# Message passing with a segment maximum: 32 of 731 row gathers taken over by TensorE's products with one-hots

## The reference

```python
x_src = x[src]; x_dst = x[dst]                       # x 6250x256 f32, 100000 edges, sorted by dst
theta_x = (x_dst - x_src) @ theta_w.T + theta_b
phi_x = x_src @ phi_w.T + phi_b
e = relu(theta_x + phi_x)
out = segment_max(e, dst, num_segments=6250)         # nodes without edges: 0
x = layernorm(x + where(isfinite(out), out, 0.0))
```

## Time and profile before

| | |
|---|---|
| median of 3 runs | 1252.21 us (1241.03 to 1252.56) |
| the profiled execution's own time | 1256.27 us |
| its span, from the first to the last instruction | 1254.5 us |
| mean granted TensorE clock | 0.574 of full speed |
| moved by DMA | 245.77 MB, 196 GB/s |

### The profile page before, as it was taken

One profiled execution on the slowest core, in us unless ns is written; L12 is line 12 of the kernel. 1 busy time (PEld: TensorE's weight loads), 2 busy tenths in 40 slices (PEclk: granted clock), 3 DMA queues, 4 the chain that ended last, 5 costly groups with the idle time before them and its releaser, 6 DMA issues.

```text
span 1254.5 us, 5930 instructions
## 1 busy us (share of the span) xinstructions
PE 302.1 (24%) x942; PEld 190.4 (15%) x953; DVE 507.1 (40%) x1155; ACT 278.6 (22%) x576; POOL 805.5 (64%) x840
## 2 busy tenths in 40 slices
PE   4165222333243323200000000010023442440000
PEld 3154111222132212100000000000011221220000
DVE  4001323455243434633334343354322542544498
ACT  1022222333232323321112121122100110111134
POOL 6713756766666667677656766767765657657574
PEclk9578555666555656555555555555555765655555
DMA  6467545666465656766656565677654756747264
GB/s 205 146 218 232 183 133 181 219 208 214 148 217 183 202 176 218 242 226 201 195 164 205 190 204 189 213 231 243 194 184 157 239 189 202 243 154 244 93 194 157
DMA packets 111585, 245.77 MB, mean 196 GB/s; under 512 B 19141, under 2 KB 51226, under 8 KB 111546
## 3 DMA queue, kind: packets, MB, share of 16 engines
q0 software_dynamic: 39984, 109.21, 30.8%
q1 hardware_dynamic: 71130, 135.51, 29.4%
q10 hardware_dynamic: 432, 0.66, 0.2%
HBM read 129.89 MB, written 115.45 MB: 196 GB/s over the span
## 4 chain that ended last, share of the span: by engine, by line
another core or an unknown queue 29%; DVE 27%; issue 21%; POOL 9%; PE 8%; ACT 4%; DMA 3%; DVEq 1%; SPq 0%; ACTq 0%; POOLq 0%
DVE acc L553 15%; POOL rows L299 9%; DVE hist L553 5%; PE ps_b L407 2%; ACT hist L359 2%; DVE stats L640 1%; DVE a_sb L629 1%; DVE hist L637 1%; PE acc L391 1%; DVE reached L559 1%; DVE a_sb L624 1%; PE ps_a L442 1%; PE ps_a L391 1%; DMA rows<-b_table,idx 1%
## 5 line engine op out<-in xcount | busy, mean ns | idle before, releaser
L299 POOL DMA_INDIRECT rows<-b_table,idx x731 | 700.0, 958 | 390.4 <-issue 216.2
L359 ACT COPY hist<-acc 128x512 f32<-128x512 f32 (+1 forms) x261 | 151.7, 586 | 497.9 <-DVE hist L553 247.1
L553 DVE SCALAR_TENSOR_TENSOR acc<-acc,reset,rows 128x256 f32<-128x256 f32 x260 | 128.2, 493 | 126.9 <-issue 46.6
L553 DVE SCALAR_TENSOR_TENSOR hist<-acc,reset,rows 128x256 f32<-128x256 f32 x261 | 126.3, 484 | 87.9 <-DVE acc L553 40.7
L553 DVE SCALAR_TENSOR_TENSOR acc<-hist,reset,rows 128x256 f32<-128x256 f32 x209 | 102.8, 492 | 136.3 <-issue 36.7
L407 PE MATMUL ps_b<-diff_sb,conv_t 128*128 128x256 f32 x204 | 89.5, 583 | 228.7 <-ACT conv_t L350 132.5
L427 PE MATMUL ps_d<-hi,row_of 128*128 128x270 bf16 (+1 forms) x89 | 43.3, 487 | 365.4 <-remote 195.7
L442 PE MATMUL ps_a<-theta_sb,xt_sb 128*128 128x256 f32 x196 | 78.3, 552 | 141.6 <-issue 89.4
L407 PEld LDWEIGHTS ps_b<-diff_sb,conv_t 128*128 128x128 f32 x204 | 52.5, 285 | 247.3 <-ACT conv_t L350 136.3
L553 DVE SCALAR_TENSOR_TENSOR acc<-hist,reset,early 128x256 f32<-128x256 f32 x51 | 25.2, 495 | 151.9 <-ACT hist L359 123.6
L364 ACT ACTIVATE signs<-ps_d,node_up 128x782 bf16<-128x782 f32 x49 | 44.7, 913 | 143.2 <-issue 72.3
(11 more groups left out here) (104 smaller groups left out, 313.7 us busy)
## 6 DMA issues: line engine op xcount, KB each, us to landing
runmax<-hist SPq DMA_DIRECT2D x260, 384.0 KB
rows<-b_table,idx POOLq DMA_INDIRECT x731
b_table<-rows SPq DMA_DIRECT2D x7, 896.0 KB, 5.5
xt_sb<-in_xt SPq DMA_DIRECT2D x49, 128.0 KB
early<-in_x SPq DMA_DIRECT2D x12, 512.0 KB
out<-hist SPq DMA_DIRECT2D x11, 512.0 KB, 2.9
xt_sb<-in_xt SPq DMA_DIRECT2D x7, 512.0 KB
xt_sb<-in_xt SPq DMA_DIRECT2D x7, 384.0 KB
```

What stands on the lines that cost most here:

```text
L299: pool.indirect_dma_start(out=rows[:, PLACE[k], :], out_offset=None, in_=b_table, in_offset=bass.IndirectOffsetOnAxis(ap=idx[:, k:k + 1], ...
L359: nc.scalar.copy(hist[:, slot:slot + n - 1, :], acc[:, at:at + n - 1, :]).then_inc(s_copied, 1)
L553: nc.vector.scalar_tensor_tensor(new, former, reset[:, k:k + 1], row_at(k), ALU.min, ALU.max).then_inc(s_fold, 1)
```

## The change

One step in 32 groups (the first step of each) is no longer gathered. It is worked out by TensorE as a product of one-hots with the table. For that the table is read back from HBM into SBUF in 25 loads of two tiles during the groups 0 to 24 and split into three bfloat16 parts whose sum is the float32 value: ScalarE rounds the first part, VectorE subtracts it, ScalarE rounds the second, VectorE subtracts that (two operations of 128x512 on each of the two engines for each load).

There are 8 products of four steps each. For a product, the 512 source numbers of its four steps are loaded to all partitions and made int16 by ScalarE. For each of the 49 tiles VectorE compares them with the tile's node numbers (128x512, int16 in, bfloat16 out), with four buffers for one-hots, and TensorE multiplies: two halves by three parts, 6 matmuls of 512 columns for each one-hot, accumulated in the two `ps_a` banks. The 49 one-hots are spread over the groups from `begin + 4` to `stop` of `PRODUCT_SPANS`: 32 groups in the first two products, 18 in the other six. VectorE makes a group's one-hots behind its three folds, and waits before each until TensorE has used the one four before it. Then ScalarE copies the product (2 copies of 128x512), TensorE turns it (8 transposes), ScalarE copies it again (2) to `far`, from where it is folded.

The tiles of A, which use the same PSUM banks, are made later and two per group, in the groups 234 to 258 in place of 204 to 252. Their first 14 loads move from the loop's start to group 232. `a_sb`, the split table and the transposed x share one area of SBUF.

The diff, without the semaphores and constants that only name things:

```diff
...
+SPLITS = 3
+AT_ONCE = 4
+HOT = 4
+PRODUCT_SPANS = ((27, 63, 8), (63, 99, 5), (99, 121, 5), (121, 143, 5), (143, 165, 5), (165, 187, 5), (187, 209, 5),
+                 (209, 231, 5))
...
+    PAIRS = (NT + 1) // 2
+    PRODUCTS = len(PRODUCT_SPANS)
+    HOT_AT = {g: [] for g in range(NG)}
+    PRODUCT_OF = {}
+    BATCH_GROUPS = []
+    for b, (begin, stop, apart) in enumerate(PRODUCT_SPANS):
+        for t in range(NT):
+            HOT_AT[begin + 4 + t * (stop - begin - 4) // NT].append((b, t))
+        first = stop + 6 if stop % 2 else stop + 7
+        BATCH_GROUPS.append([first + apart * j for j in range(AT_ONCE)])
+        for j, g in enumerate(BATCH_GROUPS[b]):
+            assert START[g] not in EARLY_OF and g < NG and (b + 1 == PRODUCTS or g < PRODUCT_SPANS[b + 1][1] + 2)
+            PRODUCT_OF[START[g]] = (b, j)
+    SPLIT_BY = PAIRS + 2
+    EVACUATE_AT = {stop: b for b, (_, stop, _) in enumerate(PRODUCT_SPANS)}
+    TURN_AT = {stop + 1: b for b, (_, stop, _) in enumerate(PRODUCT_SPANS)}
+    FAR_AT = {stop + 2: b for b, (_, stop, _) in enumerate(PRODUCT_SPANS)}
+    SOURCES_AT = {begin - 6: b for b, (begin, _, _) in enumerate(PRODUCT_SPANS)}
+    SHORT_AT = {begin: b for b, (begin, _, _) in enumerate(PRODUCT_SPANS)}
...
-    A_AT = {204 + t: t for t in range(NT)}
+    A_FROM = PRODUCT_SPANS[-1][1] + 3
+    A_AT = {A_FROM + i: [t for t in (2 * i, 2 * i + 1) if t < NT] for i in range((NT + 1) // 2)}
...
-    GATHERED = [k for k in range(STEPS) if k not in EARLY_OF]
+    GATHERED = [k for k in range(STEPS) if k not in EARLY_OF and k not in PRODUCT_OF]
...
-        xt_sb = sb("xt_sb", [P, 2 * CHUNK, KC, P])
+        shared = sb("shared", [P, NT * D * SPLITS // 2])
+        xt_sb = shared[:, 0:2 * CHUNK * D].rearrange("p (j k n) -> p j k n", k=KC, n=P)
+        split = shared[:].bitcast(BF16).rearrange("p (s t d) -> p s t d", s=SPLITS, d=D)
+        a_sb = shared[:, 0:NT * D].rearrange("p (t d) -> p t d", d=D)
+        xt_late = shared[:, NT * D:(NT + 2 * CHUNK) * D].rearrange("p (j k n) -> p j k n", k=KC, n=P)
+        assert (NT + 2 * CHUNK) * D <= NT * D * SPLITS // 2
+        work = sb("work", [P, 8 * D])
+        b_pair = work[:, 0:4 * D].rearrange("p (i j d) -> p i j d", i=2, d=D)
+        rest = work[:, 4 * D:8 * D].rearrange("p (i j d) -> p i j d", i=2, d=D)
+        turned = work[:, 0:KC * AT_ONCE * P].rearrange("p (k e) -> p k e", k=KC)
+        hot = work[:, 4 * D:4 * D + HOT * AT_ONCE * P // 2].bitcast(BF16).rearrange("p (i e) -> p i e", i=HOT)
+        assert KC * AT_ONCE * P <= 4 * D and HOT * AT_ONCE * P // 2 <= 4 * D
+        far = sb("far", [P, AT_ONCE, D])
+        sources = sb("sources", [P, AT_ONCE, P], I32)
+        short_sources = sb("short_sources", [P, 2, AT_ONCE * P], I16)
...
-            sp.wait_ge(s_bmm, NT)
-            for t in range(2 * CHUNK):
-                load_tile(t)
+            pairs = b_table.rearrange("(t p) d -> p t d", p=P)
+            by_step = src_t.rearrange("(a k) e -> a k e", a=1)
+
+            def load_pair(i):
+                if i >= 2:
+                    sp.wait_ge(s_rest, i - 1)
+                n = min(2, NT - 2 * i)
+                sp.dma_start(b_pair[:, i % 2, 0:n], pairs[:, 2 * i:2 * i + n]).then_inc(s_pair[i % 2], 16)
+
+            sp.wait_ge(s_bout[0], 16 * (CHUNKS + 1) // 2)
+            sp.wait_ge(s_bout[1], 16 * (CHUNKS // 2))
+            for i in range(2):
+                load_pair(i)
             for g in range(NG):
+                if 1 <= g < PAIRS - 1:
+                    load_pair(g + 1)
+                if g in SOURCES_AT:
+                    b = SOURCES_AT[g]
+                    if b:
+                        sp.wait_ge(s_short, b)
+                    k0, apart = START[BATCH_GROUPS[b][0]], START[BATCH_GROUPS[b][1]] - START[BATCH_GROUPS[b][0]]
+                    sp.dma_start(sources[:], by_step[:, k0:k0 + (AT_ONCE - 1) * apart + 1:apart, :].broadcast_to(
+                        [P, AT_ONCE, P])).then_inc(s_sources, 16)
+                if g == A_FROM - 2:
+                    sp.wait_ge(s_hotused, PRODUCTS * NT)
+                    for t in range(2 * CHUNK):
+                        load_tile(t)
...
-                if g in A_AT and A_AT[g] + 2 * CHUNK - 2 < NT and A_AT[g] >= 2:
-                    load_tile(A_AT[g] + 2 * CHUNK - 2)
+                if g - 1 in A_AT:
+                    for t in A_AT[g - 1]:
+                        if t + 2 * CHUNK < NT:
+                            load_tile(t + 2 * CHUNK)
...
+                if 2 <= g < PAIRS + 2:
+                    i = g - 2
+                    n = min(2, NT - 2 * i)
+                    act.wait_ge(s_rest, i + 1)
+                    nc.scalar.copy(split[:, 1, 2 * i:2 * i + n, :], rest[:, i % 2, 0:n]).then_inc(s_split2, 1)
+                if g < PAIRS:
+                    n = min(2, NT - 2 * g)
+                    act.wait_ge(s_pair[g % 2], 16 * (g // 2 + 1))
+                    nc.scalar.copy(split[:, 0, 2 * g:2 * g + n, :], b_pair[:, g % 2, 0:n]).then_inc(s_split1, 1)
...
+                if g in SHORT_AT:
+                    b = SHORT_AT[g]
+                    act.wait_ge(s_sources, 16 * (b + 1))
+                    if b >= 2:
+                        act.wait_ge(s_hot, NT * (b - 1))
+                    nc.scalar.copy(short_sources[:, b % 2, :],
+                                   sources[:].rearrange("p k e -> p (k e)")).then_inc(s_short, 1)
+                if g in EVACUATE_AT:
+                    b = EVACUATE_AT[g]
+                    act.wait_ge(s_hotused, NT * (b + 1))
+                    if b:
+                        act.wait_ge(s_turned, b)
+                    for k in range(KC):
+                        nc.scalar.copy(turned[:, k, :],
+                                       ps_a[k][:].rearrange("p j d -> p (j d)")).then_inc(s_prodev, 1)
+                if g in FAR_AT:
+                    b = FAR_AT[g]
+                    act.wait_ge(s_turned, b + 1)
+                    if b:
+                        act.wait_ge(s_fold, START[BATCH_GROUPS[b - 1][-1]] + 1)
+                    for k in range(2):
+                        nc.scalar.copy(far[:, 2 * k:2 * k + 2, :], ps_a[k][:]).then_inc(s_far, 1)
...
+                for b, t in HOT_AT[g]:
+                    i = b * NT + t
+                    if i == 0:
+                        pe.wait_ge(s_split1, PAIRS)
+                        pe.wait_ge(s_split2, PAIRS)
+                        pe.wait_ge(s_split3, PAIRS)
+                    if t == 0 and b:
+                        pe.wait_ge(s_far, 2 * b)
+                    pe.wait_ge(s_hot, i + 1)
+                    for k in range(KC):
+                        for part in range(SPLITS):
+                            mm = pe.matmul(ps_a[k][:].rearrange("p j d -> p (j d)"),
+                                           split[:, part, t, k * P:(k + 1) * P], hot[:, i % HOT, :],
+                                           start=(t == 0 and part == 0), stop=(t == NT - 1 and part == SPLITS - 1))
+                    mm.then_inc(s_hotused, 1)
+                if g in TURN_AT:
+                    b = TURN_AT[g]
+                    pe.wait_ge(s_prodev, KC * (b + 1))
+                    for j in range(AT_ONCE):
+                        for k in range(KC):
+                            mm = pe.transpose(ps_a[j // 2][:, j % 2, k * P:(k + 1) * P],
+                                              turned[:, k, j * P:(j + 1) * P], ident[:])
+                    mm.then_inc(s_turned, 1)
...
-                if g in A_AT:
-                    t = A_AT[g]
+                for t in A_AT.get(g, []):
                     pe.wait_ge(s_at[t % (2 * CHUNK)], 16 * (t // (2 * CHUNK) + 1))
+                    if t == 0:
+                        pe.wait_ge(s_far, 2 * PRODUCTS)
...
+            nc.vector.tensor_scalar(node[:], cols[:, 0:NT], float(P), part[:, 0:1], ALU.mult, ALU.add)
...
+                if k in PRODUCT_OF:
+                    return far[:, PRODUCT_OF[k][1], :]
...
+                if START[g] in PRODUCT_OF:
+                    dve.wait_ge(s_far, 2 * PRODUCT_OF[START[g]][0] + 2)
...
+                if 2 <= g < PAIRS + 2:
+                    i = g - 2
+                    n = min(2, NT - 2 * i)
+                    dve.wait_ge(s_split2, i + 1)
+                    nc.vector.tensor_tensor(split[:, 2, 2 * i:2 * i + n, :], rest[:, i % 2, 0:n],
+                                            split[:, 1, 2 * i:2 * i + n, :], ALU.subtract).then_inc(s_split3, 1)
+                if 1 <= g < PAIRS + 1:
+                    i = g - 1
+                    n = min(2, NT - 2 * i)
+                    dve.wait_ge(s_split1, i + 1)
+                    if i >= 2:
+                        dve.wait_ge(s_split3, i - 1)
+                    nc.vector.tensor_tensor(rest[:, i % 2, 0:n], b_pair[:, i % 2, 0:n],
+                                            split[:, 0, 2 * i:2 * i + n, :], ALU.subtract).then_inc(s_rest, 1)
+                for b, t in HOT_AT[g]:
```

(48 more changed lines are left out.)

2 lines of the change are left out of this document (1 added, 1 removed).

## The result

The changed kernel takes 1303.89 us (median of 4, 1296.9 to 1315.1) against 1252.38 us for the kernel before (4 runs, 1241.03 to 1255.85). The ratio is 1.0464, interval 1.0406 to 1.0522: slower by 4.6%, 51.5 us by the medians. The forecast was 1338 us with +86. Direction and main reason held; the added time came out at three fifths of the sum (51.5 of 86 us). The profiled execution took 1315.1 us.

The account below looks back on a forecast made before the run. Gathers on GpSimd set the pace, and TensorE's results arriving late under unbroken gathers take the rest. -44 + 104 + 18 + 8 = +86 us on the profiled 1256.3 gives 1342, 1338 us for the median; range 1212 to 1480 us.

Parts of the forecast that it names:

- gathers gone, split, the rest: 32 gathers less at 1.373 us, -44 us; table split in groups 0 to 24, +8; copies, turns and A tiles, 0.
- VectorE's one-hots: 392 comparisons at 0.34 us, 133 us busy, exposed only in bursts of folds: 36 us, halved to +18.
- TensorE's part: 2416 added matmuls and transposes, priced by their hand-overs under the gathers: +104 us, floor zero.
- A's pairing: Tiles of A made two per group: taken as nothing, with -20 to +50 us.
- 13 of 49 us: Share of the loop's cycle in bursts of folds, where VectorE is the bound and its one-hots cost time: 36 us.
- price by hand-overs: From stage differences, 0.26 us for each wait for TensorE; 392 + 8 of them make the 104 us taken.
- by matmuls: From the same stages, 0.086 us a matmul, 208 us for 2416; by the third stage 0.144 us, 348 us.
- Hidden: Rival: GpSimd is the only bound, TensorE's and VectorE's idle time takes the added work; -36, 1216 us; chance 0.27.
- Each matmul counts: Rival: gathers limit the number of TensorE instructions that get through; +190 to 330 us, 1442 to 1582 us; chance 0.14.
- One-hots halt GpSimd: Rival: comparisons block GpSimd's descriptor writing, 133 us on top of the gathers; +97, 1349 us; chance 0.05.
- The signs named: If right: gathers 1.6 us or more, comparison idle 100 us and more, fold waits above 115 us, TensorE in bursts.

Follow-up runs that it names:

- no products: Changed kernel with only the last of each product's 49 one-hots made and multiplied (16 matmuls, not 2352), all else kept: 1226.36 us, 0.9858 of the kernel before.
- VectorE's alone: Changed kernel with all 392 one-hots made without waiting for TensorE, which multiplies only each product's last: 1230.58 us, 0.9897 of the kernel before.
- two-of-six: Changed kernel with all one-hots and hand-overs, but 2 matmuls for each in place of 6 (first bfloat16 part only): 1266.37 us, 1.0202 of the kernel before.
- kernel with six buffers: Changed kernel with 6 one-hot buffers in place of 4: 1057.95 us, 0.976 of the kernel before (set 2); 1055.73 us, 0.9736 (set 4).
- matmuls-alone: Changed kernel with all 2352 matmuls from one constant one-hot made once, no exchange with VectorE: 1378.0 us, 1.1083 of the kernel before.
- sets 2 and 4: Experiment sets in the quick condition, both with six buffers and small early gathers: kernel before 1084.77 us (set 2) and 1083.84 us (set 4).
- set 3: Repeat of both kernels unaltered, in the slower condition: kernel before 1240.81 us, changed kernel 1299.15 us, ratio 1.0472.

## Why the prediction was right, and where its terms were off

**What bounds the kernel.** That gathers set the pace and TensorE's lateness under them takes the rest held in the condition of the result, which is the one of the trace that the forecast was read from. The cut-apart runs put the terms beside the ones priced (a few us of each are the spread of the runs, and 1302 is taken over by its ratio):

| term | priced | measured | from |
|---|---|---|---|
| gathers gone, split, the rest | -44 + 8 + 0 = -36 | -18 | before to no products |
| VectorE's one-hots | +18 | +4 | to VectorE's alone |
| TensorE's part | +104 | +72 | to the changed kernel (1302) |
| sum | +86 | +58 | 1244.67 to 1302 |

**The first term** was mis-sized by half, in several small places. The starts of the folds in one profiled execution each, before against no products, say: groups 0 to 26, with the split, 110.2 to 123.9 us, +14 for the 8 priced; groups 27 to 208, with 24 of the 32 gathers gone, 726.2 to 696.3 us, -30 for the 33 that 24 x 1.373 make; groups 209 to 260, 8 gathers gone and the tiles of A two a group, 206.4 to 202.2 us, -4 for the 11 priced, so A's pairing was perhaps not free. The first evacuations of A in the changed kernel's timeline, the answer to the earlier trace rows, show the lateness and then the run-through:

```profile
1123.07 0.76 DVE L750 TENSOR_TENSOR shared<-ps_a,bias 128x256 f32<-128x256 f32 x2 [12.30 <-remote]
1125.72 0.42 DVE L750 TENSOR_TENSOR shared<-ps_a,bias 128x256 f32<-128x256 f32 x1 [0.38 <-PE ps_a L579]
1127.43 0.42 DVE L750 TENSOR_TENSOR shared<-ps_a,bias 128x256 f32<-128x256 f32 x1 [1.28 <-PE ps_a L579]
```

**VectorE's term** failed at "13 of 49 us". The duration came out (0.34 us forecast, 0.353 in the windows, 34.64 us for 98), but with luck: at the same rate for a column, four times the 0.27 us of the earlier trace rows is 1.09, and no row shows 0.34. The share of its work that costs time is far smaller than taken: about 4 of 133 us came through, not 36 or the 18 kept of it.

**TensorE's term** had the right mechanism and the wrong unit. The step that failed is the choice of the price by hand-overs (0.26 us each) over that by matmuls (0.086 us). Hand-overs are about 0.05 us each by the equal shares of the two-of-six run, and the run without them, less its one stop, is no faster. By the same shares matmuls carry 54 of the 72 us, but at 0.023 us each, a quarter of the price worked out from the stages. A likely reason why both prices were too high, not tested, is that the earlier trace rows differ in more than TensorE's work: the first stage has 113 us of ScalarE against 79 in a stage as long. That 104 came near 72 is luck in part: the unit with the wrong mechanism had 400 pieces at five times their cost, where the right unit at its stage price would have given 208.

**The rivals.** *Hidden* (1216 us) is false in the condition of the result. In the other it fits the kernel with six buffers, where 32 gathers less at 1.25 us are 40 us and 27 and 28 were won; the groups 0 to 26 with the split take 105 and 108 us there against 88 without, which is more than the 12 or 13 missing, and groups 27 to 208, with seven of the eight products, 602 and 598 against 636. *Each matmul counts* named the mechanism better than the forecast did, but its 1442 us and more was out of reach at 0.023 us for a matmul. *One-hots halt GpSimd* fell with VectorE's alone. The rule cited of the Trainium skill (SBUF — State Buffer, 'The "DVE blocks DMA" trap (SWDGE)') did not price anything in this kernel: 967 ns for a gather with the one-hots, 960 without. No run shows whether the comparison runs in the two-port mode that the rule is about. Its other rule, in "SBUF: two separate sides", that TensorE never waits on anyone, is said of the ports of SBUF. The matmuls-alone timeline shows TensorE late by itself, sets 2 and 4 do not, and no run shows that a port is the reason, so the prediction went too far where it set its rows against that rule.

**The signs named.** The gathers reached 1.60 and 1.583 us, the first at the 1.6 named and the second just under it. The comparison's idle time is 248 us, 215 of it ending with PE or "remote" (100 named). It was 274 and 245 us in set 3's trace. GpSimd's wait for folds is 226 us (well above 115). TensorE works in bursts, and its longest wait for a one-hot is 5.6 us (5 named), but all 36 of them make only 54 us: it seldom lacked a one-hot, which speaks against hand-overs as the cost. VectorE is at 50% and did not become the bound.

## What to carry to other kernels

Before moving work from a bounding engine to an idle one, look for how the idle one gets on in stretches in which the bounding one runs without a break; its busy share says nothing of that. Price it by removing, not by comparing stages: cut-down kernels (VectorE's work alone, all hand-overs with less work) gave the terms to within some us, where stages that differ in several things gave four times the price of a matmul. An engine late by itself, with nothing to wait for, is best found by feeding it constants. And before a wait is explained by what a trace names as its end, count whether the trace has a record for each update of the semaphore.

## What the runs showed that was not expected

- With all operands at hand, a matmul of 512 columns went only every 2.1 to 2.8 us from some 15 us into an unbroken row of indirect gathers, against every 0.22 us at the row's start and once it had drained. This is the slower condition, and the cause is open.
- Removing the exchange between VectorE and TensorE made the kernel slower (1378 against 1302 us). With the exchange the lag is spread over all groups; without it, it piles up to the ends of the products, at the last into a stop of 71 us at an engine that waits in order.
- The same kernel takes 1245 or 1084 us, 15% apart, with gathers, folds and DMA packets as long as before. In the quick condition no hold-back is seen (39 to 41 evacuations in 48 us beside early gathers instead of 6 to 15), three to over five times as many semaphore records are in the trace, and ends of waits that read "remote" are replaced by the instruction that caused them: before the evacuation L438 it is "remote" for 131.5 of 174.0 us in the changed kernel, and PE's L520 for all of 106.0 with six buffers. A verdict on such a change holds for its condition.
